# First routing of a two-layer mixture-of-experts kernel: blocks grouped 1, 1, 2, 2, 2 instead of 1, 2, 2, 2, 1, and one block's conditioning issued between choice and gates

## The reference

```python
x = x + L0_ffn(L0_cond(fside, cond, x, coeffs), Wg, bg, W1, b1, W2, b2)
x = x + L1_ffn(L1_cond(x, cond, Wx, Wh, b), ln_scale, ln_bias, gate_w, Wg, Wu, Wd, sWg, sWu, sWd)
```

## Time and profile before

| | |
|---|---|
| median of 3 runs | 503.81 us (502.6 to 506.01) |
| profiled execution, its own time | 503.79 us |
| its span | 502.0 us |
| PE, DVE, ACT, POOL busy | 82%, 66%, 41%, 57% of the span |
| mean granted TensorE clock | 0.857 of full speed |

### The profile page before, as it was taken

One profiled execution on the slowest core, in us unless ns is written; L12 is line 12 of the kernel. 1 busy time (PEld: TensorE's weight loads), 2 busy tenths in 40 slices (PEclk: granted clock), 3 DMA queues, 4 the chain that ended last, 5 costly groups with the idle time before them and its releaser, 6 DMA issues.

```text
span 502.0 us, 9975 instructions
## 1 busy us (share of the span) xinstructions
PE 413.5 (82%) x2396; PEld 333.5 (66%) x2396; DVE 329.5 (66%) x1285; ACT 205.3 (41%) x651; POOL 287.0 (57%) x296
## 2 busy tenths in 40 slices
PE   5888968541999999929999999987988999999800
PEld 3554645530899999826787878776676888888700
DVE  4868785680688888712277767597478577676626
ACT  2121220500677777602555544542334455555400
POOL 2353777773377777752216676655047777776710
PEclk9857585556899999968999998997799899999955
DMA  5991111132434433114411111111313353331158
GB/s 162 310 345 48 50 52 50 53 96 63 103 107 111 110 107 97 55 56 148 132 43 39 38 39 38 38 41 41 91 45 86 106 131 101 97 102 59 49 188 330
DMA packets 48269, 49.66 MB, mean 99 GB/s; under 512 B 8747, under 2 KB 37366, under 8 KB 48086
## 3 DMA queue, kind: packets, MB, share of 16 engines
q1 hardware_dynamic: 38422, 30.04, 21.8%
q0 software_dynamic: 8640, 17.84, 10.6%
q10 hardware_dynamic: 1152, 1.14, 0.7%
HBM read 27.86 MB, written 21.12 MB: 98 GB/s over the span
## 4 chain that ended last, share of the span: by engine, by line
PE 68%; DVE 10%; POOL 7%; DMA 6%; issue 4%; SPq 1%; ACT 1%; ACTq 1%; POOLq 0%; DVEq 0%
PE banks L1156 56%; PE banks L1160 9%; POOL regions L470 4%; PE banks L1239 3%; DMA parts<-results 3%; POOL parts L457 1%; POOL results L508 1%; DMA regions<-first_w,pos 1%; DMA results<-stream,y_dest 1%; SPq L391 1%; DVE stream L764 1%; DVE parts L739 1%; POOL rstd L497 1%; DMA xpow<-in_fside_BxS 1%; DMA regions<-parts,pos 0%
## 5 line engine op out<-in xcount | busy, mean ns | idle before, releaser
L508 POOL DMA_INDIRECT results<-stream,y_dest x142 | 136.0, 958 | 75.0 <-DVE stream L959 48.5
L470 POOL DMA_INDIRECT regions<-parts,pos x64 | 64.0, 1001 | 38.2 <-issue 26.5
L470 POOL DMA_INDIRECT regions<-first_w,pos x64 | 62.7, 980 | 32.3 <-ACT hT L615 20.8
L615 ACT ACTIVATE hT<-banks,pcol 128x32 f32<-128x32 f32 x128 | 36.7, 287 | 57.5 <-PE banks L1156 56.9
L598 ACT COPY act_col<-banks 128x256 f32<-128x256 f32 x146 | 54.0, 370 | 10.5 <-PE banks L1160 9.5
L1156 PEld LDWEIGHTS banks<-hT,wh 128*128 128x128 f32 x256 | 41.7, 197 | 24.4 <-ACT hT L615 20.1
L1160 PE MATMUL banks<-const_sb,act_row 128*128 128x128 f32 x292 | 56.4, 275 | 0.0
L1036 DVE TENSOR_TENSOR act_row<-silu_row,banks 128x256 f32<-128x256 f32 x75 | 31.6, 421 | 35.7 <-ACT silu_row L669 34.0
L669 ACT ACTIVATE silu_row<-banks 128x256 f32<-128x256 f32 x75 | 28.8, 383 | 63.8 <-PE banks L1156 63.8
L1160 PEld LDWEIGHTS banks<-const_sb,act_row 128*128 128x128 f32 x292 | 41.4, 142 | 18.9 <-issue 1.7
L1156 PE MATMUL banks<-hT,wh 128*128 128x32 f32 x256 | 51.0, 282 | 1.4 <-ACT hT L615 1.4
(11 more groups left out here) (184 smaller groups left out, 844.2 us busy)
## 6 DMA issues: line engine op xcount, KB each, us to landing
parts<-results SPq DMA_DIRECT2D x16, 512.0 KB, 3.8
hT<-regions SPq DMA_DIRECT2D x71, 65.0 KB, 1.8
wgu<-regions SPq DMA_DIRECT2D x71, 65.0 KB, 1.9
results<-stream,y_dest POOLq DMA_INDIRECT x142, 2.3
base<-in_x SPq DMA_DIRECT2D x12, 128.0 KB, 3.3
regions<-const_sb SPq DMA_DIRECT2D x18, 65.0 KB, 2.7
first_w<-in_L_ffn_W SPq DMA_DIRECT2D x1, 1024.0 KB, 7.3
first_w<-in_L_ffn_W SPq DMA_DIRECT2D x2, 512.0 KB, 9.2
```

The source lines that it names most:

```text
L470: pool.indirect_dma_start(regions[layer], bass.IndirectOffsetOnAxis(ap=poss[layer][q][:, t, k:k + 1], axis=0), hrows[layer][:, q, t, k, :] ...
L508: pool.indirect_dma_start(results[layer], bass.IndirectOffsetOnAxis(ap=y_dest[:, s:s + 1], axis=0), y_row[:, s, :], None).then_inc(results ...
L615: nc.scalar.activation(hT[:, hcols(n, step_col(s), B)], rnn_ps[:, p, step_col(s):step_col(s) + B], ACT.Tanh, bias=pcol[:, ROW_CB:ROW_CB + ...
```

## The change

It regroups the blocks of the first routing. There are still five groups; their sizes go from 1, 2, 2, 2, 1 blocks to 1, 1, 2, 2, 2. And in DVE's list, `condition(2)` is issued between `choose(0, 1)` and `gates(0, 1)`, and no longer after `factors(3)`.

```diff
-GROUPS = (0,), (1, 2), (3, 4), (5, 6), (7,)
+GROUPS = (0,), (1,), (2, 3), (4, 5), (6, 7)
...
                 logits0(g)
                 choose(0, g)
+                if g == 1:
+                    condition(nexts[0])
                 gates(0, g, g % 2)
                 positions(0, g, g % 2)
                 for n in nexts[1:]:
                     factors(n)
                 for n in nexts:
-                    if n >= EARLY:
+                    if n >= EARLY and (g, n) != (1, nexts[0]):
                         condition(n)
```

## The result

The changed kernel takes 509.27 us in the median of 4 runs (509.08 to 511.08), the kernel before 503.21 us beside it (500.24 to 506.01). The ratio is 1.0121, 95% interval 1.0073 to 1.0169: slower by some 6 us. Forecast were 507.3 us, a range of 501.0 to 511.0, and "slower by over 1%" with a chance of 0.26. The time lies inside the range, but outside the band of the forecast itself (505 to 508.8), near the 510.0 of rival 2. The profiled execution took 509.35 us with a span of 507.5 us, 5.5 us over the span before.

What follows compares the result with a forecast made beforehand. POOL's 64 sends were taken to bound the first routing. Idle of 0.8 us ahead of group 1, 10.7 ahead of group 2 and 0.15 ahead of group 3, against 7.86 before, gave 503.8 + 3.5 = 507.3 us, range 501.0 to 511.0.

Steps and rivals of the forecast that it cites:

- rival 2: TensorE's clock low throughout the cycle to positions(2): 23.5 us, last send at 124.1, 510.0 us; chance 0.23.
- The frame: First routing: a change is worth only what it moves the end of POOL's last send; forecast +3.5 us.
- The signs named ahead: POOL: 8 sends from near 39.3, about 10.7 us idle, 48 unbroken sends from near 60, last end near 121.5.
- Group 1's positions: On DVE, positions(1) end at 38.4 after positions(0) at 27.43, so POOL starts group 1's sends at 39.25.
- POOL's second stop: POOL's idle time ahead of group 2, after group 1's 8 sends run out at 49.2: 10.7 us.
- The cycle: DVE and PE from end of positions(1) to end of positions(2): 20.7 us, mean of 19.89 and 21.56; the uncertain term.
- The last send of before: POOL's final send in the kernel before, taken to start at 116.98 and end at 117.94; 1.285 us a send.
- 0.15 that group 3 did not lose: POOL, free at 80.5, was to wait 0.15 us for group 3's positions, usable at 80.65.
- the bound of 1%: Smallest whole-time difference a measurement tells, 5 us; slower by more had chance 0.26, faster 0.03, within 0.71.
- Rival 1: TensorE's clock high in the cycle's first half: positions(2) at 54.6, 502.6 us, or 501.0 without ranks waits; chance 0.17.
- Part 2: condition(2) between choose and gates on DVE: costs 2.96, covers 1.8 of the ranks wait; 0 to 1.15 us lost.
- Rival 3: POOL is not what ends the first routing's stretch and nothing moves: 503.8 us; chance 0.05 together with others.

Runs made afterwards that it cites:

- e7: The changed kernel again with no edit, on another chip in a slow set; ratio 0.9951 (0.9886 to 1.0016) to the kernel before.
- e10: The changed kernel once more with no edit, in another slow set; ratio 1.0012 (0.9971 to 1.0053) to the kernel before.
- e9: Changed kernel with rows_and_logits(2) issued on PE ahead of polynomial(3); 504.24 us, ratio 0.9975 (0.9924 to 1.0027) to the kernel before.
- e5: Changed kernel's groups, but condition(2) in its old place behind factors(3), in a slow set; ratio 0.9944 (0.9887 to 1.0002) to the kernel before.
- e1: Changed kernel's groups, but condition(2) in its old place behind factors(3); ratio 1.0052 (0.9997 to 1.0108) to the kernel before.
- e11: Changed kernel's groups, but condition(2) in its old place behind factors(3), in another slow set; ratio 0.9943 (0.9900 to 0.9986) to the kernel before.

## Why the prediction was right, and where it was off

- **The frame held.** What the change is worth is what it moves the end of the sending: 3.69 of its own, where 3.5 were forecast. The signs named ahead held too: 48 unbroken sends start inside 57 to 63 (61.67), and no further stop follows.
- **Group 1's positions.** Forecast 10.97 us after positions(0), measured 11.00, and 11.02 and 11.01 in e7 and e10. The ranks came earlier than thought, at the high clock, and this changed nothing, because DVE was busy with condition(2) and the gates until 38.15.
- **POOL's second stop.** Forecast were 0.8 us ahead of group 1 and 10.7 ahead of group 2, measured 0.50 and 11.38. This is the mechanism: eight sends cover 10 us, a cycle of two blocks on PE and DVE takes 21.
- **The cycle**, taken as 20.7, measured 21.44 (39.40 to 60.84). It lay between the forecast and rival 2: polynomial(3) took the 5.49 us of low clock, the second half 9.4 us.
- **A row misread.** The last send of before was taken to be the one that starts at 116.98. It is the one at 118.24, where the chain shows its DMA. So the reference was 1.26 us too early, and a send takes 71.91 / 55 = 1.307 us, not 1.285. The 48 sends took 62.19, not 61.35. Added up: 3.5 - 1.26 + 0.84 + 0.75 for the cycle and its start - 0.15 that group 3 did not lose = 3.68. The errors nearly cancelled, and that was luck; the step was still wrong.
- **What was not in the sum**: 0.97 us ahead of the change and 0.84 us behind it. With them the profiled difference is 5.5. In the profiled pair they lift the loss over the bound of 1%, to which I had given 0.26; 3.69 us alone would be 0.7%. Single runs of the kernel before spread over 5.8 us in the first measurement and over 8.2 us in e9's set, so scatter of this size should have moved more of the chance across that line.
- **Rival 1** was half right. PE's busy stretch from 29.04 did bring the clock up (0.94 at 34 to 37), but the faster ranks and turning then only made the gap longer, 4.59 us and not 2.1, and polynomial(3) ran at 0.50. The Trainium skill (TensorE: Matmul & The Clock Gate, Part 1) says that activity releases the throttle; the trace agrees at 34 to 37 us, and shows that the gain is lost where the next work waits for another engine. Activity alone did not bring it in every execution: in e5 PE was busy without a gap from 28.30 to 36.50 and the clock stayed at 0.50. e9 reached the cycle of about 16 us that this rival had priced: 15.9 (38.40 to 54.34).
- **Part 2** was rated at 0 to 1.15 us lost. Measured up to positions(1): 1.6 where the ranks are at low clock, 2.8 where they are at high. The bound was too small because it took the low clock for the ranks as given; at the high clock there is no wait left to cover. Even at the low clock the ranks came 0.3 us earlier than reckoned. Here the number was right with luck: the sum gave the moved condition at most 1.15 of the 3.5 us and the groups the rest, and by e1 it is 2.8 for the condition and some 0.9 for the groups.
- **Rival 3** is refuted: the end of the sending moved by 4.66 us and the span by 5.5 with it, and the chain after still runs through the last send (122.90) into SP's load.

Not settled: the whole-time effect on the chips of e7 and e10, where 0 to 1% can't be told apart, and the cause of the unnamed waits there.

## What to carry to other kernels

When a queue is the bound, count its idle time in total and ask what each batch covers: here a smaller second batch started earlier and ran dry earlier, and what counted was the sum of the stops. Ask of work moved into a wait whether the wait is always there, and whether its consumer can come earlier too. Here the wait was gone when the clock was high, and z was ready 9.5 us before PE's order let it be used; moving the consumer (e9) took back 2.6 us of what the change had lost. Before taking "the last one" from a timeline, check its count and its successor in the chain.

## What the runs showed of the hardware

Two things were not expected. The first: single runs of these kernels took 500 to 511 us in the first measurement and in e9, and 570 us or more in the other four sets, the same programs among them. The chain of e1, its shares by engine, has a part that no engine of the core accounts for (7%), as e10's has; the chain of before has none.

```profile
PE 57%; DVE 12%; issue 9%; another core or an unknown queue 7%; POOL 5%; DMA 5%; ACT 3%; SPq 1%; ACTq 1%; DVEq 0%; POOLq 0%
```

The waits stand between PE and the engines that wait for its results, and POOL's sends nearly kept their pace (1.30 to 1.31 us a send in the last unbroken run of the undisturbed profiles, 1.29 to 1.42 in the others); no run here tells the cause. The second: TensorE's clock in the same stretch of the same instructions differs between executions. polynomial(2) took 4.91 us in the first profile of the changed kernel and 5.49 in e10, and the ranks behind it ran at the high clock in the one and at the low clock in the other, and with the ranks at the high clock positions(1) came 1.2 us earlier in e1 than in e5 and e11, the same program.
